# Second attention of a two-layer network on one core: products without identity and bias, in another order

## What is computed

```python
h = x * rsqrt(mean(x * x) + 1e-06) * norm_w
q, k, v = heads(Wq), heads(Wk), heads(Wv)          # of h
q, k = rope(q), rope(k)
beta, ig, og = gate(Wbeta, bbeta), gate(Wig, big), gate(Wog, bog)
def step(M, inp):
    q_t, k_t, v_t, f_t, g_t, o_t = inp
    M = M * f_t[..., None, None] + g_t[..., None, None] * scale * (k_t[..., :, None] * v_t[..., None, :])
    y_t = jnp.einsum('bhd,bhde->bhe', q_t, M) * o_t[..., None]
    return (M, y_t)
out = jnp.einsum('bld,ed->ble', y, Wout) + bout
...
x = x + _L1_attn_ref(xn, ...) + _L1_ffn_ref(xn, ...)
```

## Time and profile before

| | us |
|---|---|
| median of 3 runs | 1633.62 (1631.53 to 1633.91) |
| the profiled execution | 1643.91 |
| its span, first to last instruction | 1642.2 |
| TensorE busy | 1543.8 (94%) |
| VectorE busy | 865.9 (53%) |
| ScalarE busy | 733.1 (45%) |
| GpSimd busy | 717.8 (44%) |
| mean granted TensorE clock | 0.981 of full speed |

### The profile page before, as it was taken

The page is one execution under the profiler, slowest core; times in us unless marked ns, Lnnn a source line. Parts: engine busy times, 40 slices in busy tenths (PEclk is TensorE's granted clock), DMA queues, the critical chain, the costliest instruction groups (busy, mean ns, idle before and its releaser), DMA issues.

```text
span 1642.2 us, 32345 instructions
## 1 busy us (share of the span) xinstructions
PE 1543.8 (94%) x10802; PEld 1184.8 (72%) x10802; DVE 865.9 (53%) x2424; ACT 733.1 (45%) x1923; POOL 717.8 (44%) x815
## 2 busy tenths in 40 slices
PE   6989989999989999999997799998999999999997
PEld 3545445555547999998665467767999899999996
DVE  6777897887822444442577778874222122222220
ACT  4544545565551323323656566644333343334332
POOL 3122235666532555553810467763333433333332
PEclk9999999999999999999998999999999999999999
DMA  8533325445305343444631385367333333333331
GB/s 271 128 113 93 89 79 99 93 103 99 87 4 237 106 114 111 114 115 120 207 103 65 103 222 104 79 102 293 58 54 53 51 57 53 55 59 58 53 55 23
DMA packets 154639, 167.60 MB, mean 102 GB/s; under 512 B 84820, under 2 KB 132816, under 8 KB 151408
## 3 DMA queue, kind: packets, MB, share of 16 engines
q1 hardware_dynamic: 129936, 128.15, 30.8%
q0 software_dynamic: 24544, 37.38, 10.5%
HBM read 104.10 MB, written 44.45 MB: 90 GB/s over the span
## 4 chain that ended last, share of the span: by engine, by line
PE 68%; DVE 9%; issue 8%; POOL 8%; DMA 3%; ACT 3%; SPq 1%; DVEq 0%; POOLq 0%; ACTq 0%
PE PS L1660 23%; PE PS L1678 22%; POOL SLOT L954 6%; PE PS L1517 4%; DVE PS L1980 3%; PE PS L1453 3%; PE PS L1502 3%; PE PS L1481 2%; PE PS L1463 2%; PE PS L1543 2%; PE PS L1634 2%; PE PS L1588 2%; POOL arena L1056 1%; POOL arena L1062 1%; ACT arena L1178 1%
## 5 line engine op out<-in xcount | busy, mean ns | idle before, releaser
L1660 PEld LDWEIGHTS PS<-arena 128*128 128x128 f32 x3408 | 398.3, 193 | 16.2 <-DVE arena L2201 4.9
L1660 PE MATMUL PS<-arena 128*128 128x128 f32 x3408 | 405.3, 276 | 3.5 <-DVE arena L2201 3.5
L1678 PE MATMUL PS<-arena 128*128 x1704 | 392.3, 379 | 0.0
L1678 PEld LDWEIGHTS PS<-arena 128*128 128x128 f32 x1704 | 312.4, 190 | 39.7 <-issue 0.2
L1980 DVE CUSTOM_DVE_ANT_0 PS<-PS,arena 128x512 f32<-128x512 f32 (+3 forms) x512 | 235.4, 523 | 46.0 <-PE PS L1481 41.9
L995 POOL DMA_INDIRECT out<-arena x71 | 111.6, 1573 | 296.4 <-ACT arena L1272 274.6
L1262 ACT ACTIVATE arena<-PS,arena 128x128 f32<-128x128 f32 x568 | 161.8, 368 | 138.3 <-PE PS L1660 135.9
L2226 DVE COPY arena<-arena 128x8 f32 x71 | 12.5, 175 | 348.3 <-ACT arena L1262 326.9
L928 POOL TENSOR_SCALAR_AFFINE_SELECT arena<-arena 128x256 f32<-128x256 f32 x256 | 99.5, 412 | 206.5 <-ACT arena L1178 206.1
L981 POOL DMA_INDIRECT arena<-XN,arena x142 | 145.8, 1027 | 100.4 <-PE PS L1645 40.6
L1178 ACT ACTIVATE arena<-PS 128x512 f32<-128x512 f32 (+1 forms) x256 | 166.3, 705 | 49.5 <-PE PS L1502 39.2
(11 more groups left out here) (248 smaller groups left out, 2031.4 us busy)
## 6 DMA issues: line engine op xcount, KB each, us to landing
arena<-FD SPq DMA_DIRECT2D x32, 512.0 KB
arena<-in_w SPq DMA_DIRECT2D x16, 1024.0 KB
SPL<-arena SPq DMA_DIRECT2D x32, 384.0 KB, 2.6
arena<-SPL SPq DMA_DIRECT2D x64, 192.0 KB
XN<-arena SPq DMA_DIRECT2D x16, 512.0 KB, 3.0
arena<-SPL SPq DMA_DIRECT2D x64, 128.0 KB
arena<-SUM SPq DMA_DIRECT2D x16, 512.0 KB, 6.8
arena<-in_x SPq DMA_DIRECT2D x8, 512.0 KB, 6.8
```

The lines of the kernel that those rows point to most:

```text
L1660: ins = pe.matmul(o, m.now[i % 2][:, c * F + 128 * f:c * F + 128 * f + 128], m.xt[i % 2][:, 128 * c:128 * c + 128], start=(c == 0), stop=( ...
L1678: ins = pe.matmul(to, m.hT[i % len(m.hT)][:, 128 * c:128 * c + 128], m.WD[:, bass.ds(e * (nf * 256) + c * 256, 256)], start=(c == 0), stop ...
```

## The change

- `project_out` on TensorE issues the four instructions of y times `WOUT` only. The products with the identity and with the bias are gone, and `bias_split`, `BO3` and `ones3` with them.
- ScalarE's copy of the output is gone. A new step `out_add` on VectorE adds the output region to the tile of `ACC` and signals `oe_put`.
- A new `bias_add(b)` on GpSimd adds the bias to the four tiles of batch b in `ACC`, at the step `xa:b`, once the batch has been normalised; `out_add` waits for it (`bo_put`).
- The order: q and k of n+1, output products of n-2 (one tile later than before), values of n, turn of n. `out_add` of n-2 stands where the copy of n-1 stood, in `LATE` behind VectorE's multiplication of the affinities. The last steps run the outputs of 30 and 31 after pass 31.

```diff
-TURN = [("state", -2), ("route", 0), ("project_val", 0), ("project_qk", 1), ("turn", 0),
+TURN = [("state", -2), ("route", 0), ("project_qk", 1), ("project_out", -2), ("project_val", 0), ("turn", 0),
         ("value", 0), ("turned", 0), ("decay", 0), ("update", -1), ("rope", 1), ("affinity", 0),
-        ("sums_copy", -1), ("project_out", -1), ("keys", 0), ("weigh", 0), ("out_copy", -1), ("rope_add", 1),
+        ("sums_copy", -1), ("keys", 0), ("weigh", 0), ("rope_add", 1), ("out_add", -2),
         ("open", 1), ("decay_load", 2)]
...
-LATE = [s for s in TURN if s[0] not in ("weigh", "out_copy", "decay_load")] + [("weigh", 0), ("out_copy", -1), ("decay_load", 2)]
+LATE = [s for s in TURN if s[0] not in ("weigh", "out_add", "decay_load")] + [("weigh", 0), ("out_add", -2), ("decay_load", 2)]
...
-    out += [("rows",)] + [(kind, NT - 1) for kind in ("update", "sums_copy", "project_out", "out_copy")]
+    out += [("rows",), ("project_out", NT - 2), ("out_add", NT - 2)] + [(kind, NT - 1) for kind in ("update", "sums_copy", "project_out", "out_add")]
...
+            def bias_add(b):
+                pool.wait_ge(xn_made, b + 1)
+                four = ACC[:, 4 * b:4 * b + 4, :]
+                pool.tensor_tensor(four, four, BO.unsqueeze(1).to_broadcast([128, 4, 256]), ALU.add).then_inc(bo_put)
...
                 elif kind == "const1":
                     const1()
-                    bias_split()
+                elif kind == "xa":
+                    bias_add(*a)
...
-            def project_out(n):
-                act.wait_ge(out_made, n + 1)
-                act.activation(ACC[:, ORDER1[n], :], ps(1, 256, 512), ACT.Copy).then_inc(oe_put)
-
...
                 if n:
                     pe.wait_ge(oe_put, n)
-                else:
-                    pe.wait_ge(const1_set, 12)
-                pe.matmul(ps(1, 256, 512), ident, ACC[:, ORDER1[n], :], start=True, stop=False)
                 pe.wait_ge(yt_put, n + 1)
                 for g in range(2):
-                    pe.matmul(ps(1, 256, 512), YT[:, 128 * g:128 * g + 128], WOUT[:, g, :], start=False, stop=False)
-                pe.matmul(ps(1, 256, 512), ones3[0:96, :], BO3[0:96, :], start=False, stop=True).then_inc(out_made)
+                    ins = pe.matmul(ps(1, 256, 512), YT[:, 128 * g:128 * g + 128], WOUT[:, g, :], start=(g == 0), stop=(g == 1))
+                ins.then_inc(out_made)
...
+            def out_add(n):
+                i = ORDER1[n]
+                dve.wait_ge(bo_put, min(n + 1, NB))
+                dve.wait_ge(out_made, n + 1)
+                dve.tensor_tensor(ACC[:, i, :], ps(1, 256, 512), ACC[:, i, :], ALU.add).then_inc(oe_put)
```

More of the change, by code:

```diff
@@ L193 @@
     (-1, "keys"): "root:7",
-    (-1, "out_copy"): "scale:7 norm:7",
+    (-1, "out_add"): "scale:7 norm:7",
     (0, "turn"): "xt:7",
@@ L199 @@
     (0, "weigh"): "gates:1:0",
-    (0, "out_copy"): "logitsT:7",
+    (0, "out_add"): "logitsT:7",
     (0, "rope_add"): "logitsT_copy:7",
@@ L444, in build @@
         ID8 = view(carve(512), 512, BF16)
-        BO3 = view(carve(128), 128, BF16)
-        ones3 = view(carve(64), 64, BF16)
         assert top[0] <= hs_at
@@ L624, in build @@
         kd_put, y_made, yt_put, dm_made, m_put = (sem(n) for n in ("kd_put", "y_made", "yt_put", "dm_made", "m_put"))
-        out_made, oe_put, sums_out = (sem(n) for n in ("out_made", "oe_put", "sums_out"))
+        out_made, bo_put, oe_put, sums_out = (sem(n) for n in ("out_made", "bo_put", "oe_put", "sums_out"))
         xt_ready = {b: [(banks0[f"xt{c}", b][0], banks0[f"xt{c}", b][1] + 1) for c in range(2)] for b in range(NB)}
@@ L1062, in open_gates @@
                     pool.tensor_tensor(h8(QE2[par]), QK2[par][:, 0:8, :], hb(EF[:, i, :]), ALU.mult).then_inc(qe_put)
-            def bias_split():
-                pool.wait_ge(const1_set, 2)
-                pool.memset(ones3, 0.0).then_inc(const1_set)
-                for k in range(3):
-                    pool.wait_ge(const1_set, 3 + k)
-                    pool.memset(ones3[32 * k:32 * k + 1, :], 1.0).then_inc(const1_set)
-                pool.wait_ge(const1_set, 6)
-                pool.tensor_copy(BO3, BO).then_inc(const1_set)
-                pool.wait_ge(const1_set, 7)
-                pool.tensor_tensor(BO, BO, BO3, ALU.subtract).then_inc(const1_set)
-                for k in (1, 2):
-                    pool.wait_ge(const1_set, 7 + k)
-                    pool.tensor_copy(BO3[32 * k:32 * k + 32, :], BO[32 * k:32 * k + 32, :]).then_inc(const1_set)
-                pool.wait_ge(const1_set, 10)
-                pool.tensor_tensor(BO[64:96, :], BO[64:96, :], BO3[64:96, :], ALU.subtract).then_inc(const1_set)
-                pool.wait_ge(const1_set, 11)
-                pool.tensor_copy(BO3[64:96, :], BO[64:96, :]).then_inc(const1_set)
-                pool.wait_ge(const1_set, 12)
+            def bias_add(b):
+                pool.wait_ge(xn_made, b + 1)
+                four = ACC[:, 4 * b:4 * b + 4, :]
+                pool.tensor_tensor(four, four, BO.unsqueeze(1).to_broadcast([128, 4, 256]), ALU.add).then_inc(bo_put)
             for kind, *a in plan2:
@@ L1398, in scalar @@
                     keys(*a)
-                elif kind == "out_copy":
-                    project_out(*a)
                 elif kind == "route" and a[0] == 14:
@@ L2424, in vector @@
                     update(*a)
+                elif kind == "out_add":
+                    out_add(*a)
                 elif kind == "route":
```

## The result

The changed kernel is slower: 1651.05 us (median; 1648.31 to 1655.28), against 1635.04 for the kernel before beside it on the same chip. The ratio is 1.0089, 95% interval 1.0068 to 1.0111. That is 14.5 us above the forecast of 1636.6 and outside its range. The profiled execution took 1652.8 us (span 1651.1), against 1643.9 (1642.2). The first profile of the kernel before holds stalls of 3.5 and 3.2 us on VectorE at tiles 7 and 8 that a second profile (span 1638.5) does not show. The second in turn holds 16.0 us of waits for the loads of the decays, and the first 2.2.

A forecast was written before the change was run, and what follows sets the result against it. TensorE, without idle time, was taken to bound the attention loop. Terms +0.3 + 1.5 - 2.0 + 0.4 + 2.8 = +3.0 us took the profiled 1643.9 to 1646.9; less 10.3, the median 1636.6 us, range 1625 to 1645.

The forecast's parts named there:

- ScalarE's chain costs its 0.41 us at least once: First tiles: ScalarE's scalings and copies before the affinities leave TensorE idle, +0.41 us, entered as 0.4 in the sum.
- the term for tiles 0 to 8: First tiles of the loop, between waits on VectorE's routing: 1.7 + 0.4 + 1.4 - 1.95, taken as +1.5 us; could be -4 to +5.
- Rival 2: Loop: ScalarE's chain is covered and TensorE stays the bound, 21 periods x 0.64 less; about -10, 1623 us; chance 0.15.
- The addition on VectorE: Loop: adding 256 columns from PSUM takes 0.42 us; TensorE waits 0.13 us more before the output products.
- Tiles 9 to 23: Middle tiles of the loop: period falls from 7.05 to 6.82 to 6.95 us, gaining 1.5 to 3.5; taken as -2.0 us.
- Tiles 24 to 30: Late tiles without key products: period 6.82 to 6.95 us against 6.84; -0.1 to +0.7 over six, taken as +0.4 us.
- Those 1.95 us go: Tile 6: VectorE's 1.95 us wait for q and k, then issued after the values, disappears; credited as -1.95 us.
- q and k no longer wait behind the values: First tiles: issuing q and k ahead of the values counted as a gain; the credit for it was 1.95 us.
- The end: After the slots: output products and last addition lengthen the path to the first expert products, +2.07 and +0.8, together +2.8 us.
- Rival 4: Before the slots TensorE idles 4.9 us, then runs at half clock, as in tiles 3 and 6; 1641 to 1645 us; chance 0.18.
- Rivals 2, 3 and 5: Chain covered, 1623 us, 0.15; first tiles improve, 1630, 0.13; loop keeps 7.05 us by another wait, 1638.6, 0.04.
- The shared stage: Shared expert's stage: GpSimd's eight bias additions can each delay VectorE up to 2.3 us, mostly covered; 0 to +2, taken +0.3 us.

The follow-up runs named there:

- the two combined runs: Changed sums, q and k, values, outputs; tile 29's outputs and expert weights early: with 256 KB transfers and values first in tile 0, 1638.40 us; without these two, 1647.92 us.

## Why the prediction was wrong

The step of the mechanism that failed is "ScalarE's chain costs its 0.41 us at least once", together with the credit of 1.95 us for q and k, in the term for tiles 0 to 8. It forecast +1.5 us, and +3.5 and +5.9 were measured. More of the 14.5 us of error, 8.5, comes from carrying one execution's distance to the median over to another kernel.

- **The bound and the removed work** were read rightly. Period 6.86 against 6.82 to 6.95. With q and k between the values and the turn, as before, it is 7.04, and with the outputs there 6.43. Rival 2 had assumed that ScalarE's chain was covered; the 0.34 us show that it is not.
- **The addition on VectorE** takes 0.41 us, estimated at 0.42. TensorE idles for it 0.43 us in tiles 4, 7 and 8 and 1.67 us at the end, and not in the middle tiles, where the 0.13 us of the forecast did not appear.
- **Tiles 9 to 23**: -2.0 forecast, 15 x (7.05 - 6.86) = -2.9 where nothing stalls. Not foreseen are the waits for the decays. The earlier trace rows showed a stretch without one, and the argument took it for the whole loop.
- **Tiles 24 to 30**: +0.4 forecast from a mean of 6.84 us over six periods of the earlier trace rows. In the second profile of the kernel before five of these six periods are 6.59, and so are three in the first; the mean also held periods of 7.42, 6.87 and 6.96. Against 6.86 that is 0.27 x 6 = +1.6. This term was mis-sized by a mean.
- **Tiles 0 to 8**: +1.5 forecast, +3.5 and +5.9 measured against the two profiles of the kernel before. This is the largest of the mechanism's misses.
  - The price of the chain came from tile 31, which has state products, and was counted once. In tiles 3 to 7 it is 0.97 us of idle time each, in tiles 1 and 2 1.37 and 1.67 against 0.69 each before. The outputs as cover take 4.1 us of it away (73.6 to 69.5), with q and k still in front.
  - "Those 1.95 us go" was a wait that moved. VectorE no longer waits for q and k in tile 6, but 2.88 us for its affinities (1.82 in the second profile), against 0.62 before. The period around it is 13.88 and 12.81 us, against 13.64.
  - "q and k no longer wait behind the values" was entered as a gain. They wait for VectorE's rotation in any case, and what stands behind them waits too. In the first tile these are the values: 1.5 us, by the two combined runs, which differ in it and in the size of the transfers (13.6 and 15.1). The additions on GpSimd are the other half of the +3 there (1.4 us).
  - The other terms held. The period with the routing's count is 0.5 and 1.9 us longer, forecast 1.7. The additions on VectorE were priced about right: in the old order three of these periods are each 0.33 longer. Why that run loses nearly as much here as the whole change, with 1.7 us more in its first period, stays open.
- **The end**: +2.8 forecast. From the 31st affinities to the first expert products the kernel before takes 17.0 us (mean of two), the changed one 20.6 and 18.8: +3.6 and +1.8. Behind that come 2.3 to 2.8 us more, in the expert products at half clock. Chain and order were right, and the term misses this last part. It too may be chance: the changed kernel with the decay loads on the other queue, the same at the end, took 524.6 us from there, as the kernel before. Outputs of tile 29 ahead of the slots save 2 to 3.5 us of it.
- **Rival 4**, slower by the clock, was the nearest: 1641 to 1645 us. In both profiles the products behind the slots ran at half clock as it said, and so did those behind the waits of the first tiles. But its premise did not come: TensorE idled 2.27 us there and not 4.9, as the affinities of tile 30 came 2.5 us later and the slots at the same time. And it is no mark of the change, as the second profile of the kernel before shows the same half clock. That its figure came nearest is luck. Rivals 2, 3 and 5 fell with the period of 6.86 us and the slower first tiles.
- **The shared stage**: +0.3 forecast, +0.5 to +3.0 measured, and 87.3 us without the additions, so it is not shown that they are the cause. They cost 1.4 us in the first tile besides. The Trainium skill (SBUF — State Buffer, "SBUF: two separate sides") states that a VectorE operation with two inputs in SBUF and a GpSimd operation that reads SBUF exclude one another for the whole instruction. By the 2.35 us of the earlier trace rows the estimate was up to 18 us had all eight hit. Leaving them out gained about 4 us by the ratios, so most were covered.
- **From the profile to the median**: I kept the 10.3 us by which the profiled execution stood above the median of the kernel before. The changed kernel's profile stands 1.8 above its median. Of the 14.5 us of error 10.3 - 1.8 = 8.5 come from this step and 1652.8 - 1646.9 = 5.9 from the stages. The 5.9 look small because the stalls of that first profile stood in their base: from the second profile, 1640.3 us, the sum gives 1643.3, 9.5 us below the changed profile.

## What to carry to other kernels

Before a group is moved to the front of an in-order queue, ask what it waits for in the tiles where the other engine is late, not only in the steady tile: everything behind it inherits that wait. Here that cost 1.5 us in the first tile. Each neighbour of a step covers some latency (here one order covers ScalarE's chain, another VectorE's read of a bank), and a move has to name a new cover for each. Price a bare chain in every kind of tile: here it cost 0.34 us in the middle tiles and 0.97 where a tile has fewer products behind the turn. Take periods from undisturbed tiles, not from means, and don't carry the distance of one profiled execution to the median over to another kernel.

## What the runs showed of the hardware

- A 512 KB load broadcast from DRAM landed after 5.9 us in the median of the changed kernel and 11.3 us in a stretch with three 1 MB loads and a 1 MB store. With the load issued from another engine's queue waits of 14.7 and 12.9 us stayed, with the others cut to 256 KB 6.3 and 10.3. Without them all waits for it vanished.
- After idle times of 3.28, 3.52 and 4.57 us TensorE's next products took 3.38, 3.78 and 3.78 us, against 1.88 for the same products at full clock. But after 3.23 us in the earlier trace rows they kept full clock, and after 3.46 in the second profile of the same kernel and 2.27 at the end of the changed one they did not. The Trainium skill (TensorE: Matmul & The Clock Gate, "What's actually happening") says that activity releases the throttled state. These traces agree: after the 4.57 us in the first tile the values took 1.91 us, and those of the next tile, 7.6 us later, 1.03. They also show that an idle time of about 3 us may go either way.
- One kernel's executions differ by 7 to 9 us (1648.31 to 1655.28; 1631.53 to 1640.87), and by 19 in the largest set, 33 of the kernel before on another chip (1633.07 to 1652.38). The loop of two traces of the changed kernel differs by 14 us, along with its waits for the decays (9.3 and 21.7 us). A stage table of one profile on each side would have put such a difference down to the change. Why these waits differ from one execution to the next stays open.
